# Attention loop of a macaron block: the values matmuls moved behind the second maxima of a unit, and cut into two column halves in four of twelve units

## The reference, cut to what matters

```python
x = x + 0.5 * ffn(layernorm(x))
q, k, v = split(h @ wq.T + bq), split(h @ wk.T + bk), split(h @ wv.T + bv)   # h = layernorm(x)
scores  = where(causal, q @ k.T / sqrt(8), -inf)       # 1024 x 1024 for each batch and head
weights = softmax(scores)
x = x + (weights @ v) @ wo.T + bo
x = x + 0.5 * ffn(layernorm(x))
```

## Time and profile before

| what | us |
|---|---|
| median of 3 runs (lowest, highest) | 1035.97 (1031.82, 1037.62) |
| the profiled execution, its own time | 1038.4 |
| its span, first to last instruction | 1036.6 |
| attention loop, first score of head group 0 to first score of head group 15 | 289.55 to 789.19 |
| busy in the span: PE, DVE, ACT, POOL | 831.8, 601.5, 523.4, 489.6 |
| granted PE clock, mean over the span | 0.89 |

### The profile page before, as it was taken

One profiled execution on the slowest core, in us unless ns is written; L12 is line 12 of the kernel. 1 busy time (PEld: TensorE's weight loads), 2 busy tenths in 40 slices (PEclk: granted clock), 3 DMA queues, 4 the chain that ended last, 5 costly groups with the idle time before them and its releaser, 6 DMA issues. The chain is left out here.

```text
span 1036.6 us, 18080 instructions
## 1 busy us (share of the span) xinstructions
PE 831.8 (80%) x6599; PEld 446.5 (43%) x6599; DVE 601.5 (58%) x1237; ACT 523.4 (50%) x841; POOL 489.6 (47%) x686
## 2 busy tenths in 40 slices
PE   8569999944668988888978899878887618999990
PEld 7437878742212223332333323323232316787770
DVE  7931211124767788888787977878775423334235
ACT  6323343442237776777556786566766303433330
POOL 5047455325652662646467522562224651545453
PEclk9769999986657999999799999999899758999995
DMA  7115575621451262341524224323202124423236
GB/s 204 73 26 153 148 217 145 192 63 51 130 162 66 53 189 48 89 144 43 174 76 105 99 53 152 85 65 106 53 18 79 53 63 149 130 79 97 78 136 228
DMA packets 96185, 110.81 MB, mean 107 GB/s; under 512 B 12279, under 2 KB 68763, under 8 KB 96104
## 3 DMA queue, kind: packets, MB, share of 16 engines
q1 hardware_dynamic: 84752, 88.86, 29.1%
q0 software_dynamic: 9216, 17.98, 6.8%
q10 hardware_dynamic: 2136, 2.91, 0.8%
HBM read 57.86 MB, written 52.89 MB: 107 GB/s over the span
## 5 line engine op out<-in xcount | busy, mean ns | idle before, releaser
L1903 DVE TENSOR_REDUCE m_blk<-banks 128x8 f32<-128x1024 f32 (+1 forms) x320 | 348.5, 1114 | 79.7 <-PE banks L1505 67.1
L1823 ACT ACTIVATE pt<-banks 128x1024 f32<-128x1024 f32 (+3 forms) x384 | 300.4, 811 | 145.1 <-PE banks L1489 142.7
L1537 PE MATMUL banks<-pt,vs 128*32 128x512 f32 (+3 forms) x1536 | 176.6, 534 | 7.2 <-POOL pt L2252 3.8
L1489 PE MATMUL banks<-qb,kp 64*128 64x512 bf16 (+3 forms) x768 | 132.6, 351 | 53.7 <-DVE m_blk L1903 45.2
L2252 POOL TENSOR_SCALAR_AFFINE_SELECT pt<-pt 128x512 f32<-128x512 f32 x128 | 81.6, 637 | 192.1 <-ACT pt L1823 191.7
L1505 PE MATMUL banks<-kp,qa 64*128 64x128 bf16 (+4 forms) x1152 | 126.4, 294 | 19.6 <-ACT pt L1823 11.6
L849 POOL DMA_INDIRECT xe<-xn_rows,slot_tok x80 | 79.9, 999 | 94.4 <-PE banks L1190 37.2
L675 POOL DMA_INDIRECT y_tab<-ys,ids x70 | 68.0, 972 | 81.5 <-DVE ys L635 64.5
L1106 ACT ACTIVATE he<-banks,b_up 128x512 f32<-128x512 f32 (+1 forms) x96 | 57.9, 616 | 89.9 <-PE banks L1190 89.5
L1505 PEld LDWEIGHTS banks<-kp,qa 48*128 48x128 bf16 (+1 forms) x1152 | 46.2, 99 | 130.3 <-ACT pt L1823 92.7
L585 ACT ACTIVATE hT<-banks,bfc 128x512 f32<-128x512 f32 (+1 forms) x96 | 56.3, 615 | 84.9 <-DVE bfc L607 48.8
(11 more groups left out here) (344 smaller groups left out, 1128.8 us busy)
## 6 DMA issues: line engine op xcount, KB each, us to landing
bucket<-zero SPq DMA_DIRECT2D x16, 660.0 KB
qb<-q_stack SPq DMA_DIRECT2D x32, 192.0 KB, 3.5
qa<-q_stack SPq DMA_DIRECT2D x30, 192.0 KB, 3.3
kp<-k_stack SPq DMA_DIRECT2D x30, 192.0 KB, 4.2
q_stack<-qp SPq DMA_DIRECT2D x18, 256.0 KB
k_stack<-kq SPq DMA_DIRECT2D x18, 256.0 KB
y_slots<-ye SPq DMA_DIRECT2D x16, 256.0 KB, 2.5
mid<-x SPq DMA_DIRECT2D x8, 512.0 KB, 3.6
```

The source lines that it names most:

```text
L1489: i = nc.tensor.matmul(ring[SLOT["score", 2 * u + pair]][:, s, 0:w], kp[g][rows_s, pair, kb * P:(kb + 1) * P], qb[par][rows_s, pair, q0:q0 ...
L1537: i = nc.tensor.matmul(o_bank[VW * h:VW * h + VW, q:q + w], vs[par][:, kb, h, :], pt[u % PTS][:, h, 0:w], start=u in (0, SECOND), stop=u i ...
L1823: nc.scalar.activation(pt[u % PTS][:, 2 * pair:2 * pair + 2, 0:w], ring[SLOT["score", 2 * u + pair]][:, :, 0:w], ACT.Exp, scale=SCALE).the ...
L1903: nc.vector.tensor_reduce(dst, ring[slot][:, :, 0:blocks * P].rearrange("p s (j k) -> p s j k", k=P), AX.X, ALU.max).then_inc(m_done, 1)
```

## The change

In `step` of PE's program, `values` is called behind the second maxima of a unit instead of between the second score and the second maxima. In units 7 to 10 of all head groups but the last it is called twice: its left 256 columns behind the first maxima, its right 256 behind the second. `values` gets the argument `half` for this; its waits are made with the left half, its signal with the right one. Units 2, 3 and 11 have no second maxima, so their order stays.

```diff
-                def values(par, n, u):
+                def values(par, n, u, half=None):
...
+                    c0, c1 = (0, w) if half is None else (half * w // 2, (half + 1) * w // 2)
+                    if half == 1:
+                        pass
+                    elif u in (0, SECOND):
                         wait(pe, o_done, 2 * n + u // SECOND)
...
-                        i = nc.tensor.matmul(o_bank[VW * h:VW * h + VW, q:q + w],
-                                             vs[par][:, kb, h, :], pt[u % PTS][:, h, 0:w],
+                        i = nc.tensor.matmul(o_bank[VW * h:VW * h + VW, q + c0:q + c1],
+                                             vs[par][:, kb, h, :], pt[u % PTS][:, h, c0:c1],
                                              start=u in (0, SECOND), stop=u in (SECOND - 1, NU - 1))
-                    i.then_inc(pv_done, 1)
+                    if half != 0:
+                        i.then_inc(pv_done, 1)
...
+                    IN_HALVES = (7, 8, 9, 10)
...
                             score(par, g, n, u, pair)
-                            if pair == 1:
+                            if more and m0 + pair < m1:
+                                slot_free(("max", m0 + pair), n, more, first)
+                                maxima(ng, nb, m0 + pair, SLOT["max", m0 + pair])
+                            if u in IN_HALVES and more and (u >= LAG or not first):
+                                values(*((par, n, u - LAG) if u >= LAG else (1 - par, n - 1, NU - LAG + u)), pair)
+                            elif pair == 1:
                                 if u >= LAG:
                                     values(par, n, u - LAG)
                                 elif not first:
                                     values(1 - par, n - 1, NU - LAG + u)
-                            if more and m0 + pair < m1:
-                                slot_free(("max", m0 + pair), n, more, first)
-                                maxima(ng, nb, m0 + pair, SLOT["max", m0 + pair])
```

More of the change, by code:

```diff
@@ L1520, in uses_of @@
                     return 2 * b + g // 2 + 1
-                def values(par, n, u):
+                def values(par, n, u, half=None):
                     hf, kb = UNITS[u]
                     q0, w = unit_queries(u)
-                    if u in (0, SECOND):
+                    c0, c1 = (0, w) if half is None else (half * w // 2, (half + 1) * w // 2)
+                    if half == 1:
+                        pass
+                    elif u in (0, SECOND):
                         wait(pe, o_done, 2 * n + u // SECOND)
@@ L1530, in values @@
                             pe.wait_ge(v_copied, n + 1)
-                    if u in MASKED:
+                    if half == 1:
+                        pass
+                    elif u in MASKED:
                         pe.wait_ge(masked, len(MASKED) * n + MASKED.index(u) + 1)
```

## The result

Twelve runs of each kernel: before 1036.22 us median (1027.17 to 1039.86), changed 1042.74 us (1039.97 to 1049.09). The ratio is 1.0087 with a 95% interval of 1.0058 to 1.0117, so the change makes the kernel slower by 6.5 us in the medians. The forecast was 1043.3, range 1030 to 1053.

The account below looks back on a forecast made before the run. PE was taken as the bound, busy 80% and waiting mostly for reductions, then exponentials. Terms of 23.3 us lost and 16.0 gained sum to +7.3, giving 1045.7 for the profiled execution and 1043.3 against the median; range 1030 to 1053.

Parts of the forecast that it names:

- 8 head group 0: Head group 0, which has long waits at the lower clock: -1.0 us.
- The two patterns: Without side task, second score waits for a reduction, values inside that loop; with reductions on time, values fill ACT's exponential time.
- the floor of 1.57: Least time in us from a unit's first score to its second maxima, whose slot the first score's exponential must free.
- Term 1: Units 0 and 1: unit 0 loses 0.58, later waits take up part; +3.4 us over 14 head groups.
- Terms 2 and 3: Units 4 and 5: values put between second maxima and side task, +10.2 us; unit 6, whole values likewise exposed, +5.9.
- Term 4: Units 7 to 10 of g = 1: right halves lengthen the loop of projection, ACT and maxima; +3.8 us.
- Term 5: Units 7 to 10 of head groups 2, 3, 7, 11, 13, without side tasks: halves fit into gaps; -9.0 us.
- Term 6: Units 7 to 10 of g = 0: DVE full in head groups 4 and 8, -0.1 each; head group 12 -0.7; -0.9 us.
- Term 7: Units 6 to 10 of g = 2 with a router: earlier maxima shorten DVE's queue and PE's wait; -5.1 us.
- The waits: PE's waits for ACT before maxima grow from 11.6 to some 30 us; for DVE before scores fall from 45.2 to under 25.
- The delays of units 4 and 5: Rival: later waits absorb the values put into units 0, 1, 4 and 5; 13.6 us vanish, 1030 us; chance 0.2.
- The clock did not fall clearly more often: Rival: longer PE waits in units 0, 4, 5, 6 make the clock fall more often; 1053 us; chance 0.15.

Follow-up runs that it names:

- (b): Against the changed kernel: values back ahead of the second maxima in all units but 7 to 10, which stay cut; 1023.07 us, ratio 0.9896 to the kernel before.
- (c): Changed kernel with ACT's exponential of each first score taken over the left half of its columns alone; 1008.29 us, with 1031.32 for the kernel before.
- (f): Against (b): right half in units 7 to 10 placed between second score and second maxima; 1021.69 us, ratio 0.9852 to the kernel before.
- the repetition: The changed kernel run once more, nothing changed; 1042.51 us, ratio 1.0058 to the kernel before.
- (e): Against (b): units 7 and 8 of g = 1 uncut, unit 6 of head groups 6, 10, 14 with whole values behind second maxima; 1020.32 us, ratio 0.9841.

## Why the prediction was right

The start-to-start lengths of all units, after less before, put together by the terms of the sum. They come from one profile of each kernel, and so contain what the clock did in these two:

| term | forecast | measured |
|---|---|---|
| 1 units 0 to 3 | +3.4 | +0.6 |
| 2 units 4 and 5 | +10.2 | +12.0 |
| 3 unit 6 without the router groups | +5.9 | +6.9 |
| 4 units 7 to 11, g = 1 | +3.8 | +2.4 |
| 5 units 7 to 11, free | -9.0 | -8.1 |
| 6 units 7 to 11, g = 0 | -0.9 | -2.6 |
| 7 units 6 to 11, router groups | -5.1 | -6.3 |
| 8 head group 0 | -1.0 | -1.4 |
| sum | +7.3 | +3.5 |

**The two patterns** held to a few hundredths: 2.46 for a cut unit (2.47 said), 3.15 for unit 4 and 3.98 for unit 6 of head group 4 (3.15 and 3.99 said). (b) shows that they are separate outside the router groups, (c) that ACT's exponential makes the floor of 1.57, and (f) that a half in DVE's loop costs time again in units 8 and 10.

**Term 1** was set too high as a sum of this pair. In the eight head groups with an undisturbed unit 0 it is +0.29 in seven (0.35 said), unit 0 losing 0.57 and unit 2 giving back 0.33. In five of the other six they even got shorter, most in head groups 11 and 13 (1.7 and 1.4), whose unit 2 had lasted 4.4 and 4.5 before, where 2.9 is the rule. Head group 4, the eighth, got longer by 1.7. Such shifts need not return: in the repetition head group 4 was shorter again by 1.4 us in units 1 and 2, and unit 2 of head group 11 lasts 2.95 in (b) and (e), whose code is that of the kernel before there. By the means of all profiles terms 1 and 2 together are +11.6, for 13.6 forecast.

**Terms 2 and 3** are a little over. Units 4 and 5 lose 0.92 to 0.94 where 0.95 was said; the router groups 0.6, 1.4 and 1.7. At the full clock their unit 5 with its logits went from 3.88 to 4.23; in head groups 10 and 14 of the changed kernel's profile it took 4.66 and 4.96, because the clock fell inside it (mean 0.90 and 0.84). Unit 6 of a free head group lasts 3.02, not 2.89, because its exponential stands behind the read of `o_bank` in ACT, which I had left out there.

**Term 4**: units 7 and 8 lose 0.57 each as said, but unit 9 gives 0.35 back. (e) shows the other side of it: with units 7 and 8 uncut again, unit 9 lasts 3.73 instead of 3.20. The two units are coupled to unit 9.

**Term 5** is short by 0.9. Head groups 3 and 13 gave 2.0 each (1.8 said), but 7 and 11 only 1.2, because their unit 8 lasts 3.39 and 3.40 and not 2.57. PE waits there for POOL, which makes the transposed row maxima ready, and POOL is still busy with DMA issues of the experts (L404). I had not looked at POOL for these units. Head group 7:

```profile
552.83 0.97 POOL L404 DMA_INDIRECT bucket<-rows,row_ix  x1 [0.30 <-issue]
553.82 0.30 POOL L2236 TENSOR_SCALAR m_neg<-m_of 128x16 f32<-128x16 f32 x1
...
555.39 0.22 PE L1554 MATMUL banks<-identb,m_parts 128*48 128x128 bf16 x1 [0.77 <-POOL m_parts L2240]
```

**Term 6** was mis-sized. I held DVE to be full in units 7 to 10 of head groups 4 and 8 and gave them 0.1; they gave 0.83 each, 0.49 of it in unit 8, which now runs at the floor of a cut unit (2.57). So DVE left more room there than its mean busy share suggests. **Term 7** is near as a sum, but not in its working: units 6 and 7 together gave -1.3, -0.6 and -0.8 in head groups 6, 10 and 14 (-1.4 said), and the units behind gave -2.0, -0.8 and -0.8 (-0.3 said). The -2.0 is in part the clock of the kernel before, which was at the lower level in units 5 to 9 of head group 6. With the repetition in place of the first profile the term is -4.7.

**The waits** moved the way that was said but further: 58.4 and 8.3 us, where I had said some 30 and under 25. In unit 4 of head group 4 the wait rose by 0.56, which is the whole length of the values, and so it is in each such unit; I had added these lengths up for the time but not for the waits. Of the head groups, 1, 5 and 9 grew by 3.4, 2.4 and 2.4 (3 said); 7, 11 and 13 shrank by 1.4, 1.4 and 2.9 (1 to 2 said), but head group 2 did not: its unit 6 took 4.07, with the clock at 0.72, where 3.02 is the length at the full clock.

**The rivals.** The delays of units 4 and 5 were not taken up: +12.0 stayed of them. The clock did not fall clearly more often: ten times in the loop of the changed kernel and eight in its repetition, for nine before, with a mean over the loop of 0.94 for 0.93. It fell at other places, though, and the price that I gave a fall was too high. Of the 3.75 us between head groups 13 and 2, 1.73 lie in unit 0, where the clock was 1.00 and PE waited for DVE; the fall behind it, 6.8 us long, took the other 2.0, and I had set 2 for one of 3.4. The fall in units 1 and 2 of head group 4 cost 1.4 us, by the repetition that has none there, and the one in unit 6 of head group 2 cost 1.1.

As to the rule on short idle times that the forecast cited from the Trainium skill ("TensorE: Matmul & The Clock Gate", section "A second HAM failure mode: psum-queue depth-cycling"): the clock does swing in both kernels, and I did not test why. The change is no test of the rule either. PE's idle time in the loop grew from 75.0 to 79.4 us only, since the waits for DVE went down as those for ACT went up.

**What stays open** is the size beyond the loop. The one profiled pair differs by 2.4 us, the medians of 12 by 6.5, the two ratios say 0.9% and 0.6%. The twelve executions of the changed kernel spread over 9 us, and there is one profile of the kernel before, so I can't say how much of the rest is the clock. By the profiled loop (+3.5) my sum of +7.3 was twice too high, mostly by terms 1 and 6; by the medians (+6.5) it was nearly exact, and that is in part luck, as terms 1, 4 and 6 came out below the forecast and terms 2 and 3 above it. The direction, and what happens in each kind of unit, are shown; the last 3 us are not.

## What to carry to other kernels

In a ring of slots with two readers, each filler between two writes is either inside the loop of one reader or in the shadow of the other. Work out for each the time from its slot's write to its release, and put the filler before the write that waits last. Moving the filler behind a write is free only if that write was not waiting; otherwise its whole length is added. Cutting a filler in two is worth its extra fixed cost where there are two gaps (here 0.14 for 0.57), but each half must be placed by the wait of its own unit: one rule for all units lost here what a rule by unit won.

## What the runs showed of the hardware

The lengths of units repeated from one execution to the next to a few hundredths of a microsecond (166 of 191 within 0.03), while the 22 whole executions of that program spread from 1033 to 1049 us. Within the profiled loop, what varies is gathered in a few units, most of them with a granted clock below 1.00: 3.71 us at 0.61 and 2.56 at 1.00 for the same unit. In both kernels the clock fell in unit 1 or 2 of head groups 5, 9 and 13 and in units 5 or 6 of head groups 6, 10 and 14. Cut in two, a group of 8 matmuls of 512 columns (1.00 from start to next start) became two of 0.57 each (414.99 to 415.56, and 416.35 to 416.92), so the fixed part of a group was paid twice nearly in full.
